# The first of two layers by a seven-product scheme, with its output kept in DRAM before the second layer

## The chip, the cores and the metric

The kernel runs on one core of one Trainium2 chip. The metric is the device time of one execution in microseconds. Five engines work side by side, each through its own list of instructions in order: TensorE (PE; PEld is its weight load), VectorE (DVE), ScalarE (ACT), GpSimd (POOL) and SyncE (SP, which here only issues DMAs). They wait for each other by semaphores.

## The reference

```
x: (8, 256, 1024) f32;  W0: (1024, 1024);  Wr: (8, 1024);  A: (8, 16, 1024);  B: (8, 1024, 16);  W1: (16, 1024, 1024)
logits = x @ Wr.T, plus 5 at expert lang_id[b];  gates = softmax of the two largest, 0 elsewhere
x1  = x  + x @ W0.T + 2 * sum over experts e of gates[e] * (x @ A[e].T) @ B[e].T
out = x1 + x1 @ W1[adapter[b]].T
```

Everything is f32. There are 2048 tokens of 1024 features. The two large products, x by W0 (the first layer) and x1 by the W1 that a row of 256 tokens picks (the second), have 2048 x 1024 x 1024 multiplications each.

## The kernel before

f32 operands are cut into a high part in fp32r and a low part (value minus high part), and a product is three matmuls: high by high, high by low, low by high. `load` (L244) brings a tile of 128 x 1024 numbers with four DMAs of 128 KB, each into 32 partitions (L255). GpSimd adds the identity to each weight tile (`add_ones`, L301, a 128x128 block), which gives the residual. VectorE transposes the tile (`turn`, L349), ScalarE copies out the high part (`high`, L487) and VectorE subtracts it from the tile (`low`, L356). A ring of four raw tiles and one of two turned tiles lie between them.

The work goes in four chunks of 512 tokens (two rows), by a loop of three turns and a last one written out. In each chunk TensorE makes `features` (x by A and Wr; L577 with 272 columns, L579 with 136), then eight `base_tile`s of 24 matmuls 128x512 each for W0 (L564 to L566) with `lora_tile`s of three, and then the second layer: eight output tiles of 24 matmuls, with x1 still in SBUF. From `features` VectorE works out the gates (`make_gates`, L398 to L436) and TensorE turns the gated features (L611). x1 leaves PSUM by `x1_high` (L507) and `x1_low` (L443). `put_out` (L517, L523) copies an output tile and stores it. W0 is loaded anew in each chunk, so the weights have 96 tiles in all (32 of W0, 64 of W1). The order of loads is a table (`FIRST`, `AFTER_GATES`, ..., `after_l1`).

Of the kernel before, what the change touches and what calls it, by code (L numbers as in the profile page):

```python
# [5 lines left out]
def cond_resid_kernel(nc, x, lang_ids, adapter_ids, w0, wr, a, b, w1, out):  # L25
    F32 = mybir.dt.float32
# [26 lines left out]

    WPC = M + BPC * M
    GROUPS = 3
    RING = GROUPS * KH
    RAW = 4
    BANKS = 7

    WARM = 37  # L60
    OUTS = 4
    L1_OUTS = NH * TT
    assert WPC % RING == 0 and ER == P and L1_OUTS % OUTS == 0 and M == 8 and L1_OUTS == 8

    AHEAD = 3
    FIRST = [("x", 0), ("a", 0)] + [("x", j) for j in range(1, XT)] + [("w", 0), ("w", 1), ("w", 2), ("b", 0)]
    AFTER_GATES = [("w", 3), ("w", 4)]
    AFTER_GATED = [("w", 5), ("w", 6), ("w", 7)]  # L70
    AFTER_L0 = [[], [], [("w", 8), ("w", 9)], [("w", 10), ("w", 11)], [("w", 12), ("w", 13)], [("w", 14), ("w", 15)],
                [("w", 16), ("w", 17)], []]

    def after_l1(j, last):
        own = [[18, 19], [20, 21], [22, 23], []][j]
        tokens = [[0, 1], [2, 3], [], []][j]
        following = [[], [], [0, 1], [2]][j]
        return [("w", n) for n in own] + ([] if last else [("x", t) for t in tokens] +
                                          [("w", WPC + n) for n in following])

    def body_order(last):
        return (AFTER_GATES + AFTER_GATED + [t for l in AFTER_L0 for t in l] +
                [t for j in range(NH) for t in after_l1(j, last)])
# [17 lines left out]
    with ctx:  # L101
# [564 lines left out]
```

## Time and profile before

| | us |
|---|---|
| median of 3 runs (lowest, highest) | 424.11 (423.76, 424.12) |
| the profiled execution, its span | 423.0 |
| PE busy / PEld busy | 414.4 / 349.1 |
| DVE busy | 314.1 |
| ACT busy | 163.1 |
| POOL busy | 59.5 |
| DMA | 68.52 MB, 162 GB/s over the span |

The profiled execution has only its span as a time of its own; it is 1.1 us shorter than the median of the runs. Busy time of PE counts overlapping matmuls, each of which is recorded at about 390 ns though the next starts earlier: the work of PE is read from the distance between starts.

### The profile page before, as it was taken

The numbers are of one execution on the slowest core, as the hardware profiler recorded it, in microseconds if no ns is written. First come the engines' busy times: TensorE is split into PE (matmuls) and PEld (weight loads), VectorE is DVE, ScalarE is ACT, GpSimd is POOL, SyncE is SP. The second block draws the span as 40 slices with busy tenths as digits, with TensorE's granted clock in tenths as the row PEclk, the third lists the DMA queues.
The fourth block names the chain that finished last, engine by engine and source line by source line (L and its number), as shares of the span: only waits on it lengthen the run. The fifth ranks groups of instructions, "written<-read, shape, count | busy, mean of one in ns | idle before, by whom it ended". The sixth has DMA issues, their size and how long they took to land.

```text
span 423.0 us, 6707 instructions
## 1 busy us (share of the span) xinstructions
PE 414.4 (98%) x1978; PEld 349.1 (83%) x1978; DVE 314.1 (74%) x378; ACT 163.1 (39%) x192; POOL 59.5 (14%) x104
## 2 busy tenths in 40 slices
PE   8898999999999999999999999999999999999996
PEld 8786888888898888888888888888889888888885
DVE  3999999999307999998615799999830799994410
ACT  3432544555212455454321445455421245533321
POOL 1021211201200121012110022111310012221000
PEclk9999999999999999999999999999999999999999
DMA  7994677797913666699650576679960356654111
GB/s 173 232 219 120 167 190 200 212 259 203 225 47 99 150 187 180 161 260 249 173 132 0 153 181 188 170 218 252 243 160 26 99 151 175 189 161 123 51 50 50
DMA packets 82542, 68.52 MB, mean 162 GB/s; under 512 B 7986, under 2 KB 82258, under 8 KB 82514
## 3 DMA queue, kind: packets, MB, share of 16 engines
q1 hardware_dynamic: 65618, 59.84, 55.3%
q10 hardware_dynamic: 16896, 8.39, 7.3%
q8 instruction: 8, 0.13, 0.1%
q14 instruction: 20, 0.16, 0.1%
HBM read 59.81 MB, written 8.39 MB: 161 GB/s over the span
## 4 chain that ended last, share of the span: by engine, by line
PE 89%; DVE 3%; DMA 2%; SPq 2%; issue 2%; ACT 0%; POOL 0%; DVEq 0%; ACTq 0%; POOLq 0%
PE banks L564 28%; PE banks L565 28%; PE banks L566 28%; PE banks L577 4%; SPq L255 2%; PE banks L579 1%; DMA raw<-in_L_cond_W_dram 1%; DMA raw<-in_x_dram 1%; DVE turned L349 1%; DVE turned L345 0%; DVE w_lo L356 0%; POOL raw L301 0%; PE gT_ps L611 0%; ACT w_hi L487 0%; DVE gT_lo L449 0%
## 5 line engine op out<-in xcount | busy, mean ns | idle before, releaser
L356 DVE TENSOR_TENSOR w_lo<-turned,w_hi 128x1024 fp32r<-128x1024 f32 x96 | 118.8, 1259 | 38.8 <-ACT w_hi L487 38.0
L487 ACT ACTIVATE w_hi<-turned 128x1024 fp32r<-128x1024 f32 x96 | 101.5, 1062 | 113.1 <-DVE turned L349 103.3
L349 DVE STREAM_TRANSPOSE turned<-raw 128x1024 f32<-128x1024 f32 x113 | 135.3, 1225 | 10.1 <-DMA raw<-in_x_dram 5.1
L301 POOL TENSOR_TENSOR raw<-raw,ident 128x128 f32<-128x128 f32 x96 | 58.4, 608 | 325.9 <-DMA raw<-in_L_cond_weight_dram 182.7
L564 PE MATMUL banks<-xT_hi,w_hi 128*128 128x512 f32 x256 | 100.2, 391 | 0.0
L565 PE MATMUL banks<-xT_lo,w_hi 128*128 128x512 f32 x256 | 99.7, 389 | 0.0
L566 PE MATMUL banks<-xT_hi,w_lo 128*128 128x512 f32 x256 | 99.6, 389 | 0.0
L564 PE MATMUL banks<-w_hi,x1T_hi 128*128 128x512 f32 x256 | 99.6, 389 | 0.0
L565 PE MATMUL banks<-w_lo,x1T_hi 128*128 128x512 f32 x256 | 99.6, 389 | 0.0
L566 PE MATMUL banks<-w_hi,x1T_lo 128*128 128x512 f32 x256 | 99.6, 389 | 0.0
L566 PEld LDWEIGHTS banks<-xT_hi,w_lo 128*128 128x128 f32 x256 | 48.1, 188 | 10.0
L564 PEld LDWEIGHTS banks<-w_hi,x1T_hi 128*128 128x128 f32 x256 | 48.1, 188 | 10.0
L565 PEld LDWEIGHTS banks<-w_lo,x1T_hi 128*128 128x128 f32 x256 | 48.1, 188 | 10.0
L566 PEld LDWEIGHTS banks<-w_hi,x1T_lo 128*128 128x128 f32 x256 | 48.1, 188 | 9.9
L565 PEld LDWEIGHTS banks<-xT_lo,w_hi 128*128 128x128 f32 x256 | 48.1, 188 | 9.7
L564 PEld LDWEIGHTS banks<-xT_hi,w_hi 128*128 128x128 f32 x256 | 48.1, 188 | 9.7
L517 ACT ACTIVATE out_stage<-banks 128x512 f32<-128x512 f32 x32 | 19.1, 597 | 71.3 <-PE banks L566 71.3
L577 PE MATMUL banks<-fac,xT_hi 128*128 128x272 f32 x128 | 30.7, 335 | 2.0 <-DVE fac L389 1.9
L579 PE MATMUL banks<-fac,xT_lo 128*128 128x136 f32 x128 | 29.0, 226 | 0.0
L577 PEld LDWEIGHTS banks<-fac,xT_hi 128*128 128x128 f32 x128 | 24.1, 188 | 2.5 <-DVE xT_lo L356 2.4
L443 DVE TENSOR_TENSOR x1T_lo<-banks,x1T_hi 128x512 fp32r<-128x512 f32 x32 | 21.2, 682 | 5.4 <-ACT x1T_hi L507 5.4
L398 DVE TENSOR_TENSOR h<-banks,h 128x544 f32<-128x544 f32 x4 | 2.9, 719 | 29.5 <-ACT h L499 29.5
(54 smaller groups left out, 197.8 us busy)
## 6 DMA issues: line engine op xcount, KB each, us to landing
raw<-in_L_cond_weight_dram SPq DMA_DIRECT2D x256, 128.0 KB, 2.7
raw<-in_L_cond_W_dram SPq DMA_DIRECT2D x128, 128.0 KB, 3.5
raw<-in_x_dram SPq DMA_DIRECT2D x64, 128.0 KB, 3.3
out_dram<-out_stage ACTq DMA_DIRECT2D x32, 256.0 KB, 3.1
raw<-in_L_cond_A_dram SPq DMA_DIRECT2D x4, 128.0 KB, 3.1
raw<-in_L_cond_B_dram SPq DMA_DIRECT2D x4, 128.0 KB, 4.5
gated<-in_L_cond_Wr_dram SPq DMA_DIRECT2D x4, 8.0 KB
lang_i<-in_itok_B_dram SPq DMA_DIRECT2D x1, 4.0 KB, 2.9
```

The lines of the kernel that those rows point to most:

```text
L255: sp.dma_start(raw[c * S:(c + 1) * S, s, :].rearrange("p (q j) -> p q j", q=Q), src[:, :, c * DQ:(c + 1) * DQ]).then_inc(raw_loaded[s], 16)
L301: nc.gpsimd.tensor_tensor(spot, spot, ident[:].rearrange("p (q j) -> p q j", q=Q), ALU.add)\
L349: nc.vector.transpose(turned[:, slot(item, ch, last, 2)].rearrange("p m (q s) -> p q m s", q=Q), raw[:, s, :].rearrange("p (q m j) -> p q ...
L356: nc.vector.tensor_tensor(dest(False, item), turned[:, slot(item, ch, last, 2)], dest(True, item).bitcast(F32), ALU.subtract)\
L443: nc.vector.tensor_tensor(x1T_lo[:, k, :], banks[:, l0_bank(k), :], x1T_hi[:, k, :].bitcast(F32), ALU.subtract).then_inc(x1_done, 1)
L487: nc.scalar.activation(dest(True, item), turned[:, slot(item, ch, last, 2)], ACT.Copy)\
L517: nc.scalar.activation(out_stage[:, s, :].rearrange("p (q k s) -> p q k s", q=Q, k=KH), banks[:, l1_bank(n), :].rearrange("p (k q s) -> p ...
L564: nc.tensor.matmul(ps, st_hi, mv_hi, start=start, stop=False)
L565: nc.tensor.matmul(ps, st_hi, mv_lo, start=False, stop=False)
L566: return nc.tensor.matmul(ps, st_lo, mv_hi, start=False, stop=stop)
L577: nc.tensor.matmul(banks[:, j, 0:2 * FC], xT_hi[:, m, t], fac[:, m, :, :].rearrange("p s f -> p (s f)"), start=m == 0, stop=False)
L579: mm = nc.tensor.matmul(banks[:, j, 0:FC], xT_lo[:, m, t], fac[:, m, 0, :], start=False, stop=m == M - 1)
```

## The change

The first layer is made once for the whole W0, in two spans of 1024 tokens. W0 (transposed, features by outputs) and the span's x are each cut into four quarters of 512 x 512. Four sums of W0's quarters (s1 to s4) and four of x's (t1 to t4) are formed, and seven products of quarters take the place of eight; `ORDER` gives their order. The products 1 and 2 use quarters without a sum; 6 is s2 by t2, 7 is s3 by t3, 5 is s1 by t1, 4 a quarter of W0 by t4, 3 is s4 by a quarter of x. With a for W0 and b for x the sums are s3 = a11 - a21, s2 = a22 - s3, s1 = a21 + a22, s4 = a12 - s2, t1 = b12 - b11, t2 = b22 - t1, t3 = b22 - b12, t4 = b21 - t2. All are made by GpSimd, with 128x512 instructions: 16 for W0, 16 for the x of each span. The four quarters of x1 come out of PSUM by further copies and additions (`copy_p1`, `copy_u2`, `copy_u3`, `add_p1`, `add_up`), are cut into high and low part in a stage of two places, and are written to a DRAM tensor `x1_kept` (`keep`). The second layer follows after both spans, row by row: `load_x1` reads a row's high and low parts back with two DMAs of 1 MB, issued by ScalarE; W1's tiles come through five raw places and three groups of four tiles. `features` is now one f32 matmul of 136 columns per block in place of the two fp32r ones. The loops are written out.

```diff
+    ORDER = (1, 2, 6, 7, 5, 4, 3)
...
+    LOADS = ([("a",)] + [x_item(0, 0, t) for t in range(XT)] + [("w", m) for m in range(HM)] +
+             [x_item(0, 1, t) for t in range(XT)] + [("w", m) for m in range(HM, M)] + [("b",)] +
+             [x_item(1, h, t) for h in range(2) for t in range(XT)])
...
+    x1_kept = nc.dram_tensor("x1_kept", [M, P, 2, NB * T], F32, kind="Internal").ap()
...
+            def keep(s, quarter, r):
+                e = quarter_at(s, quarter, r)
+                m = r + (HM if quarter[0] == "2" else 0)
+                t0 = s * 2 * HALF + (HALF if quarter[1] == "2" else 0)
+                sp.wait_ge(x1_lo_done, e + 1)
+                sp.dma_start(x1_kept[m, :, :, t0:t0 + HALF], stage[:, e % 2].rearrange("p (h f) -> p h f", h=2))\
+                    .then_inc(kept[e % 2], 16)
...
+            def make_t1(s, t):
+                pool.wait_ge(transposed, TURN_AT[x_item(s, 1, t)] + 1)
+                pool.wait_ge(featured, featured_at(s, 0, t) + 1)
+                pool.wait_ge(lo_done, PIECE_AT[("x", 1, 1, HM - 1) if s else ("xt", t)] + 1)
+                nc.gpsimd.tensor_tensor(half_x(0, t, 0), half_x(1, t, 0), half_x(0, t, 0), ALU.subtract)\
+                    .then_inc(t1_done, 1)
...
+            def make_s3(r):
+                pool.wait_ge(transposed, TURN_AT["w", HM + r] + 1)
+                pool.wait_ge(lo_done, PIECE_AT["wt", r] + 1)
+                a11, a21 = quarter_w(7, r), quarter_w(5, r)
+                nc.gpsimd.tensor_tensor(a11, a11, a21, ALU.subtract).then_inc(s3_done, 1)
+            def make_s2(r):
+                pool.wait_ge(s3_done, r + 1)
+                nc.gpsimd.tensor_tensor(s2_sum(r), quarter_w(4, r), quarter_w(7, r), ALU.subtract).then_inc(s2_done, 1)
+            def make_s1(r):
+                a21, a22 = quarter_w(5, r), quarter_w(4, r)
+                nc.gpsimd.tensor_tensor(a21, a21, a22, ALU.add).then_inc(s1_done, 1)
+            def make_t2(s, k):
+                if s == 0:
+                    pool.wait_ge(t1_done, k + 1)
+                    dst, b22, t1 = t2_by_tile(k, 1, ring_f), half_x(1, k, 1), half_x(0, k, 0)
+                    b22, t1 = (v.rearrange("p (m f) -> p m f", m=HM) for v in (b22, t1))
+                else:
+                    pool.wait_ge(t1_done, 2 * XT)
+                    pool.wait_ge(steps, k_end(*UNITS[UNIT_AT[1, 6, k, 1] - RING][0:3]))
+                    dst, b22, t1 = unit(1, 6, k, 1, ring_f), quarter_x(1, HM + k), quarter_x(0, k)
+                nc.gpsimd.tensor_tensor(dst, b22, t1, ALU.subtract).then_inc(t2_done, 1)
+            def make_t4(s, k):
+                pool.wait_ge(t2_done, s * HM + k + 1)
+                if s == 0:
+                    t2, b21 = t2_by_tile(k, 1, ring_f), half_x(0, k, 1).rearrange("p (m f) -> p m f", m=HM)
+                else:
+                    t2, b21 = unit(1, 6, k, 1, ring_f), quarter_x(0, HM + k)
+                nc.gpsimd.tensor_tensor(b21, b21, t2, ALU.subtract).then_inc(t4_done, 1)
+            def make_s4(r):
+                pool.wait_ge(s2_done, r + 1)
+                a12 = quarter_w(3, r)
+                nc.gpsimd.tensor_tensor(a12, a12, s2_sum(r), ALU.subtract).then_inc(s4_done, 1)
+            for m in range(HM):
+                add_ones(("w", m))
+            for t in range(XT):
+                make_t1(0, t)
+                make_t2(0, t)
+                make_t4(0, t)
+            for r in range(HM):
+                add_ones(("w", HM + r))
+                make_s3(r)
+                make_s2(r)
+                make_s4(r)
+            for t in range(XT):
+                make_t3(0, t)
+            for r in range(HM):
+                make_s1(r)
+            for t in range(XT):
+                make_t1(1, t)
+            for t in range(XT):
+                make_t3(1, t)
+            for k in range(HM):
+                make_t2(1, k)
+                make_t4(1, k)
+            for n in range(NW1):
+                add_ones(("w1", n))
...
+            def load_x1(row):
+                if row == 0:
+                    act.wait_ge(steps, product_end(1, 4))
+                elif row == 1:
+                    act.wait_ge(steps, product_end(1, 3))
+                else:
+                    act.wait_ge(l1_ready, (row - 1) * 2 * TT)
+                for slot in range(2):
+                    act.wait_ge(kept[slot], (8 if row < NB // 2 else 16) * 16)
+                for low in range(2):
+                    act.dma_start(x1_part(row, low).bitcast(F32),
+                                  x1_kept[:, :, low, row * T:(row + 1) * T].rearrange("m p t -> p m t"))\
+                        .then_inc(x1_loaded[row % 2], 16)
...
+            def step(s, i, k, r, bank, first):
+                ps = bank.rearrange("p (t f) -> p t f", t=XT)
+                u_hi, u_lo = (u_part(i, r, low)[:, k * P:(k + 1) * P] for low in range(2))
+                x_hi, x_lo = x_part(s, i, k, 0), x_part(s, i, k, 1)
+                nc.tensor.matmul(ps, u_hi, x_hi, start=first and k == 0, stop=False, skip_group_check=True)
+                nc.tensor.matmul(ps, u_hi, x_lo, start=False, stop=False, skip_group_check=True)
+                nc.tensor.matmul(ps, u_lo, x_hi, start=False, stop=k == HM - 1, skip_group_check=True)\
+                    .then_inc(steps, 1)
...
+            def span(s):
+                product(s, 6, lambda r: pe.wait_ge(p1_copied, HM * s + r + 1), False, main_bank)
+                turn_gated(s)
+                product(s, 7, lambda r: pe.wait_ge(u2_copied, HM * s + r + 1), False, main_bank, range(HM - 1))
+                pe.wait_ge(gT_done, s + 1)
+                pe.wait_ge(lo_done, PIECE_AT["b",] + 1)
+                for r in range(HM):
+                    pe.wait_ge(p1_added, HM * s + r + 1)
+                    lora(s, "11", r)
+                product(s, 7, None, False, main_bank, range(HM - 1, HM))
+                product(s, 5, lambda r: pe.wait_ge(summed_up, added_at(s, "11", r) + 1), True, side_bank)
+                for r in range(HM):
+                    lora(s, "22", r)
+                product(s, 4, lambda r: pe.wait_ge(u3_copied, HM * s + r + 1), False, main_bank)
+                for r in range(HM):
+                    lora(s, "21", r)
+                product(s, 3, lambda r: pe.wait_ge(summed_up, added_at(s, "22", r) + 1), False, side_bank)
+                pe.wait_ge(lo_done, PIECE_AT["bd",] + 1)
+                for r in range(HM):
+                    lora(s, "12", r)
...
+            features(0, 0)
+            for _ in range(FILL):
+                nc.tensor.matmul(banks[:, 0, 0:P], ident[:], ident[:], start=True, stop=True)
+            first_products()
+            span(0)
+            features(1, 0)
+            features(1, 1)
+            product(1, 1, lambda r: pe.wait_ge(summed_up, added_at(0, "12", r) + 1), True, main_bank)
+            product(1, 2, lambda r: pe.wait_ge(h_copied, 3 + r // 2), True, side_bank)
+            span(1)
```

GpSimd, at the start. Before, it only adds the identity to weight tiles (`raw`), three of them ahead of the loop:

```order
L285 IOTA iota_i 128x8
L287 AFFINE_SELECT ident<-ident 128x128
L301 TENSOR_TENSOR raw<-raw,ident 128x4x32 x3
L311 UNCONDITIONAL_BRANCH
L311 ISA
L301 TENSOR_TENSOR raw<-raw,ident 128x4x32 x3
```

After; `tokens_f` is x transposed, `ring_f` holds t2, `turned_w_f` W0 transposed, `weights_f` s2 (the rows begin with the first four weight tiles and end within the second one of the other four):

```order
L490 TENSOR_TENSOR tokens_f<-tokens_f,ring_f 128x512
L451 TENSOR_TENSOR tokens_f<-tokens_f 128x512
L482 TENSOR_TENSOR ring_f<-tokens_f 128x4x128
L490 TENSOR_TENSOR tokens_f<-tokens_f,ring_f 128x512
L444 TENSOR_TENSOR raw<-raw,ident 128x4x32
L463 TENSOR_TENSOR turned_w_f<-turned_w_f 128x512
L467 TENSOR_TENSOR weights_f<-turned_w_f 128x512
L495 TENSOR_TENSOR turned_w_f<-turned_w_f,weights_f 128x512
L444 TENSOR_TENSOR raw<-raw,ident 128x4x32
L463 TENSOR_TENSOR turned_w_f<-turned_w_f 128x512
```

Between the identity of W0's fourth tile and that of the fifth there are now twelve sums of x, and between the fifth and the sixth three sums of W0.

ScalarE, in the second layer. Before, between two output tiles (`out_stage` to DRAM) it makes high parts for W and x:

```order
L517 ACTIVATE out_stage<-banks 128x512
L523 ISA
L523 DMA out_dram<-out_stage 512x1x128
L476 REGISTER_ALU
L487 ACTIVATE xT_hi<-turned 128x8x128
L476 REGISTER_ALU
L487 ACTIVATE xT_hi<-turned 128x8x128
L515 REGISTER_ALU
L517 ACTIVATE out_stage<-banks 128x512
L523 ISA
L523 DMA out_dram<-out_stage 512x1x128
```

After; `tokens<-x_kept` are the two DMAs that read a row of x1 back:

```order
L948 ACTIVATE turned_w<-weights_f 128x8x128 x2
L959 ACTIVATE sums<-banks 128x512
L965 DMA out_dram<-sums 512x1x128
L937 DMA tokens<-x_kept 128x8x256 x2
L948 ACTIVATE weights<-weights_f 128x8x128 x2
L959 ACTIVATE sums<-banks 128x512
L965 DMA out_dram<-sums 512x1x128
L948 ACTIVATE weights<-weights_f 128x8x128 x2
```

A row's x1 is now asked for on ScalarE's queue behind the last output tile of the row two before it.

## Rows read from the trace of the kernel before

**Rows 1.** The page, part 1 (engine, busy us, share), and the PEclk row

```profile
PE 414.4 (98%) x1978; PEld 349.1 (83%) x1978; DVE 314.1 (74%) x378; ACT 163.1 (39%) x192; POOL 59.5 (14%) x104
PEclk9999999999999999999999999999999999999999
```

**Rows 2.** The page, part 4: the chain that ended last, shares by engine

```profile
PE 89%; DVE 3%; DMA 2%; SPq 2%; issue 2%; ACT 0%; POOL 0%; DVEq 0%; ACTq 0%; POOLq 0%
```

**Rows 3.** Timeline of PE, second layer: start, length (us), what; 44 matmuls between

```profile
104.56 0.39 PE L564 MATMUL banks<-w_hi,x1T_hi 128*128 128x512 f32 x1
...
114.76 0.39 PE L564 MATMUL banks<-w_hi,x1T_hi 128*128 128x512 f32 x1
```

**Rows 4.** Timeline of PE, features: first pair, and the one seven pairs later

```profile
14.82 0.39 PE L577 MATMUL banks<-fac,xT_hi 128*128 128x272 f32 x1 [1.89 <-DVE fac L389]
15.10 0.34 PE L577 MATMUL banks<-fac,xT_hi 128*128 128x272 f32 x1
...
16.76 0.33 PE L577 MATMUL banks<-fac,xT_hi 128*128 128x272 f32 x1
```

**Rows 5.** Windows of L561: stretch, length, PE busy (records), PEld, PEclk, DMA, GB/s

```profile
3.00:5.00 2.00, 2.00 (x11) 2.00 (x11) 1.00 0.79 188
9.00:11.00 2.00, 2.00 (x21) 2.00 (x20) 1.00 0.93 188
```

**Rows 6.** The chain of waits in order of time, its end: start, length, what

```profile
419.05 0.24 PE banks L566
419.31 0.60 ACT out_stage L517
```

**Rows 7.** The chain of waits, the turning of the gated features

```profile
136.12 0.44 PE gT_ps L611 x4
```

**Rows 8.** Groups of instructions by form: count | busy us, mean ns | idle before

```profile
L349 DVE STREAM_TRANSPOSE turned<-raw 128x1024 f32<-128x1024 f32 x113 | 135.3, 1225 | 10.1 <-DMA raw<-in_x_dram 5.1 <-DMA raw<-in_L_cond_A_dram 1.4 <-POOL raw L301 1.2
L356 DVE TENSOR_TENSOR w_lo<-turned,w_hi 128x1024 fp32r<-128x1024 f32 x96 | 118.8, 1259 | 38.8 <-ACT w_hi L487 38.0
L301 POOL TENSOR_TENSOR raw<-raw,ident 128x128 f32<-128x128 f32 x96 | 58.4, 608 | 325.9 <-DMA raw<-in_L_cond_weight_dram 182.7 <-DMA raw<-in_L_cond_W_dram 143.3
L443 DVE TENSOR_TENSOR x1T_lo<-banks,x1T_hi 128x512 fp32r<-128x512 f32 x32 | 21.2, 682 | 5.4 <-ACT x1T_hi L507 5.4
L507 ACT ACTIVATE x1T_hi<-banks 128x512 fp32r<-128x512 f32 x32 | 18.0, 591 | 13.9 <-PE banks L566 13.9
L283 POOL MEMSET gated<- 128x256 f32 x1 | 0.3, 312 | 0.3 <-POOLq L653 0.3
L284 POOL MEMSET ident<- 128x128 f32 x1 | 0.2, 206 | 0.0
```

**Rows 9.** GpSimd line L301: duration ns min/median/max

```profile
L301 POOL TENSOR_TENSOR raw<-raw,ident x96: 454/464/1471, 17.8 to 385.5; 128x128 f32<-128x128 f32 x96
```

**Rows 10.** Timeline of all engines, start

```profile
1.68 11.25 PE L561 MATMUL gT_ps<-ident 128*128 128x128 f32 x74 [1.68 <-POOL ident L287]
5.10 1.25 DVE L349 STREAM_TRANSPOSE turned<-raw 128x1024 f32<-128x1024 f32 x1 [5.10 <-DMA raw<-in_x_dram]
11.93 1.85 SPq L255 DMA_DIRECT2D raw<-in_L_cond_W_dram  x4
17.82 0.58 POOL L301 TENSOR_TENSOR raw<-raw,ident 128x128 f32<-128x128 f32 x1 [16.19 <-DMA raw<-in_L_cond_W_dram]
```

**Rows 11.** Timeline of DVE, gates of the third chunk

```profile
227.28 0.19 DVE L400 TENSOR_TENSOR logits<-h,bias 128x32 f32<-128x32 f32 x1 [0.16 <-DVE h L398]
227.62 0.36 DVE L408 MAX8 top<-logits 128x8 f32<-128x8 f32 x4
230.29 0.69 DVE L436 TENSOR_TENSOR gated<-h,gates 128x512 f32<-128x512 f32 x1
```

**Rows 12.** Windows of all engines; DMA share and GB/s stand last

```profile
13.00:22.00 9.00, 7.05 (x57) 6.90 (x58) 8.63 (x9) 3.44 (x4) 1.37 (x2) 1.00 1.12 232
88.00:94.00 6.00, 6.00 (x28) 4.97 (x27) 5.79 (x6) 3.67 (x4) 0.00 (x0) 1.00 1.07 256
108.00:111.00 3.00, 3.00 (x15) 2.49 (x14) 0.26 (x1) 0.00 (x0) 0.46 (x1) 1.00 0.97 289
```

More of the change, by code:

```diff
@@ L55, in cond_resid_kernel, with x_item @@
+    def x_item(s, h, t):
+        return ("x", s, h, t)
     GROUPS = 3
[L56 to L60, printed above, removed]
+    NW1 = NB * M
+    L1_OUTS = NB * 2 * TT
     OUTS = 4
[L62 to L70, printed above, removed]
@@ L281, in _ @@
+            load_w1(10)
+            keep(1, "12", 2)
+            load_w1(11)
+            keep(1, "12", 3)
+            for n in range(12, NW1):
+                load_w1(n)
         @block.gpsimd
@@ L372, in _ @@
+            turn(x_item(0, 0, 1))
+            low(("xt", 0))
             dve.wait_ge(consts, 3)
@@ L459, in _ @@
[L459 to L465 removed]
+            turn(x_item(0, 0, 3))
+            low(("xt", 2))
+            turn(("w", 0))
+            low(("xt", 3))
+            turn(("w", 1))
+            low(("wt", 0))
+            turn(("w", 2))
+            low(("wt", 1))
+            turn(("w", 3))
+            low(("wt", 2))
@@ new lines, in _ @@
+            span(0)
+            low(("x", 1, 1, 0))
+            low(("x", 1, 1, 1))
+            turn(x_item(1, 1, 0))
+            for r in range(HM):
+                add_up(0, "12", r)
+            turn(x_item(1, 1, 1))
+            x1_low(0, "12", 0)
+            x1_low(0, "12", 1)
+            turn(x_item(1, 1, 2))
+            low(("x", 1, 1, 2))
+            low(("x", 1, 1, 3))
+            turn(x_item(1, 1, 3))
+            x1_low(0, "12", 2)
+            x1_low(0, "12", 3)
+            make_gates(1)
@@ new lines, in highs, with copy_h @@
+            def highs(kind, *which):
+                for r in range(HM):
+                    high((kind, *which, r))
+            def copy_h(s, h):
+                act.wait_ge(featured, featured_at(s, h, XT - 1) + 1)
+                if s:
+                    for slot in range(2):
+                        act.wait_ge(kept[slot], 8 * 16)
+                nc.scalar.activation(h_all[:, h * XT:(h + 1) * XT, :].rearrange("p (k i) f -> p k (i f)", i=2),
+                                     features_of(s, h), ACT.Copy).then_inc(h_copied, 1)
@@ new lines, in _ @@
+            span(0)
+            high(("x", 1, 1, 0))
+            high(("x", 1, 1, 1))
+            x1_high(0, "12", 0)
+            x1_high(0, "12", 1)
+            high(("x", 1, 1, 2))
+            high(("x", 1, 1, 3))
+            x1_high(0, "12", 2)
+            x1_high(0, "12", 3)
+            copy_h(1, 0)
+            copy_h(1, 1)
+            exponentials(1)
+            highs("x", 1, 2)
+            for r in range(HM):
+                copy_p1(1, r)
+            high(("x", 1, 6, 0))
+            high(("x", 1, 6, 1))
@@ new lines, in _ @@
+            high(("x", 1, 6, 2))
+            high(("x", 1, 6, 3))
+            high(("x", 1, 7, 0))
+            high(("x", 1, 7, 1))
+            for r in range(HM):
+                copy_u2(1, r)
+            gT_high(1)
+            high(("x", 1, 7, 2))
+            high(("x", 1, 7, 3))
+            span(1)
+            high_w1(5)
+            load_x1(1)
+            x1_high(1, "12", 0)
+            x1_high(1, "12", 1)
+            high_w1(6)
+            high_w1(7)
+            x1_high(1, "12", 2)
```

1174 lines of the change are left out of this document (763 added, 411 removed).

## The prediction

> **What bounds the kernel now.** I read the page first. TensorE is busy 98% of the span and VectorE 74% [rows 1]; the chain that ended last runs through PE for 89% [rows 2]. So nearly each microsecond is TensorE's work, and what TensorE does not have to do comes off the time, as long as it is fed. Two matmuls overlap in the records, so the price of one is the distance between starts: 45 steps from 104.56 to 114.76 us, 0.2267 us for 512 columns [rows 3]. A pair of the features' matmuls takes (16.76 - 15.10) / 7 = 0.237 us [rows 4]. TensorE begins its features at 14.82 us [rows 4] and ends at 419.3 [rows 6]; 3.7 us of store follow to 423.0. Its work sums to 1632 x 0.2267 = 370.0, 128 x 0.237 = 30.3 and 16 turns at 0.11 = 1.8 [rows 7], 402.1 us in all, so in those 404.5 us it stood still only 2.4. The start, 14.8 us, and that are all that a better feed could win.
>
> **TensorE's work after.** Seven products in two spans are 7 x 2 x 4 x 4 x 3 = 672 matmuls of 512 columns where 768 were: 672 x 0.2267 = 152.3 us. The LoRA keeps its 96 (21.8), the second layer its 768 (174.1), the turns 1.8. The features become 128 f32 matmuls of 136 columns. An f32 matmul leaves two records, and 21 of 128 columns start in 2.00 us [rows 5]: 0.095 per record, 0.19 to 0.20 per matmul, 0.21 for 136 columns, 27.2 us in all. The sum is 377.2 us, 24.9 less. That is the whole gain.
>
> **The start: GpSimd's sums.** Product 6 cannot start before s2 of all four row blocks, and nothing is queued on TensorE that could go ahead of it. What lies before it on TensorE is features (6.8), product 1 (10.9), features (6.8), product 2 (10.9): 35.4 us.
>
> Loads. The first tile is turned from 5.10 to 6.35 us [rows 10]. With three raw slots a slot is used again after 1.85 us of issue, the landing (issued by 13.78, seen by GpSimd at 17.82: 4.04) [rows 10] and a turn of 1.25: about 7.3 us for three tiles, 2.45 each. x's fifth tile is the tenth loaded: 6.35 + 9 x 2.45 = 28.4 us. The last x tile follows at about 36, so product 1 ends near 32 and product 2 near 49.
>
> The price of a sum of 512 columns on GpSimd is in no row. The nearest is L301, 128 columns, 454 ns at least and 608 on average [rows 8, 9]. From below: two memsets of 256 and 128 columns take 312 and 206 ns [rows 8], 100 ns of which is fixed; if 200 were fixed here, 512 columns would cost 0.20 + 4 x 0.254 = 1.22 us. From above: 4 x 0.454 = 1.82, or 4 x 0.608 = 2.4 when VectorE gets in the way (a record of 1471 ns shows that it can) [rows 9]. With 100 ns fixed it is 0.10 + 4 x 0.354 = 1.52, and I take 1.5, the overhead nearest to a row.
>
> The Trainium skill (GPSIMD Engine Reference, Elementwise: side-by-side cycle accounting) states about 2.6 cycles an element at 1.2 GHz for two inputs. By it this sum would cost an estimated 1.1 us plus dispatch, and the chain below would be about 7 us shorter; L301's 454 ns for 128 columns, with the same rate, leaves 0.18 us for dispatch, so the row doesn't contradict it.
>
> GpSimd's queue, in order, from 28.4 us: 12 sums of x; then for each of W0's last four row blocks the identity (0.46), the turn on VectorE that waits for it (1.25, with 0.2 of signals), and s3, s2, s4, which wait for that turn; the next identity is queued behind s4. Up to the last s2 that is 12 + 3 x 3 + 2 = 23 sums, 34.5 us, four times 1.91 = 7.6, and 23 signals of about 0.05: 43.3. s2 is ready at 71.7; ScalarE's high part (0.59) and VectorE's low part (0.68) [rows 8] with signals bring 73.3 us. TensorE has been idle since 49, for 24 us.
>
> After such a rest the clock. After the rest ahead of the program only 11 records of L561 start in 2 us where later 21 do [rows 5], though the profile gives a granted clock of 1.00, its 2.4 GHz level, in both. All 74 take 11.25 us [rows 10], and would take 74 x 0.095 = 7.0 at the later pace: a restart costs at most 4.2 us, at least nothing if the clock holds. I charge 3.0. Product 6 ends at 73.3 + 10.9 + 3.0 = 87.2. The gates of 1024 tokens wait for product 7's first pieces, which wait for t3, behind the last s4: 71.7 + 5 x 1.5, 79.5, and 2 us of cutting. The chunk's gates take 3.7 us [rows 11], with twice as many maxima and indices about 5.2: done at 86.9, just covered by product 6.
>
> **The rest of the first layer.** In span 0 VectorE has per product about four sums from PSUM, four low parts of x1, four of W0 and four of x: 16 x 0.68 = 10.9 us against 13.6 of TensorE (a product with its LoRA), so it keeps up with little to spare; without W0's parts in span 1, more. Stage and `kept` waits add a few microseconds where VectorE and ScalarE are in order behind a store, and the second gates have 10.9 us of product 1 to hide in and need 10 to 12. I charge 3.0 us for all of that. The copies on ScalarE (12 per span at 0.59) and the second half of GpSimd's sums lie beside products. W0 being loaded once (24 tiles less for VectorE, 60 us) is worth nothing, as VectorE was not the bound.
>
> **The second layer: DMA.** It now has no first layer between to fetch in. A row has 96 matmuls, 21.8 us, for which come 4.19 MB of W1, 2.10 of x1 and 1.05 of output: 7.34 MB, 337 GB/s. When it starts nine W1 tiles have been brought; up to its last group it still needs 55 tiles (28.8 MB), seven rows of x1 (14.7), the last four `keep`s (2.1) and 28 outputs (7.3), 52.9 MB. Of its 174.1 us, 159 are left for that when the last group (10.9) and some 4 us of landing, turning and cutting are taken off: 333 GB/s to be hidden. The rows show: loads alone 232 GB/s with the DMA engines full (share 1.12), loads with stores 256 at a share of 1.07, and 289 at 0.97 for 3 us [rows 12]. From below 256 gives 52.9 / 0.256 + 15 = 222 us, 48 more than TensorE's. From above 289 x 1.12 / 0.97 = 334 hides it all. I take 289 / 0.97 = 298, the mixed stretch that is nearest to this traffic, taken to a full engine: 177.5 + 15 = 192.5 us, 18.4 more. VectorE needs 2 x 1.24 us per tile, 8 tiles in 19.9 us of a row's 21.8, and is not the bound.
>
> The Trainium skill (DMA: Bandwidth & Descriptors, Measured) gives 341 GB/s for a transfer of 1 MB, the size of `load_x1`'s. By it x1's 14.7 MB would take an estimated 43 us in place of 49 and the layer 6 us less; no row here shows so large a transfer.
>
> **The sum.** 73.3 + (377.2 - 35.4 = 341.8) + 3.0 + 3.0 + 18.4 + 3.7 = 443.2 us against the execution's own 423.0; the runs' median lies 1.1 above it: **444 us**.
>
> **Rivals.**
> (a) The sums as above, but the second layer keeps TensorE's pace. For it: the loads' 232 GB/s go into 32 partitions at a time, and x1 comes over all 128; a stretch with stores was already at 289. Against it: 333 was held nowhere. 444 - 18.4 = 425.6 us, within 5 of it.
> (b) Faster: the 24.9 us of matmuls saved outweigh the late start. It is one mechanism, a sum at its lower price on GpSimd, and it counts only where (a) holds too: with 1.22 us the chain is 23 x 0.28 = 6.4 us shorter, 419.2 us. It decides below 1.43 us a sum (425.6 - 424.1 = 1.5 us, over 23). For it speaks the L301 median of 464 ns, hardly above its minimum; against it that VectorE is denser at the start than elsewhere.
> (c) Both go badly: GpSimd and VectorE shut each other out (L301 at 608 on average, 1.3 times its median, which makes a sum 1.95 us and the chain 10 us longer), or DMA stays at 256 GB/s (30 more): 454 to 480 us, 465 as its middle.
>
> **Chances.** Forecast 0.50; (a) 0.22; (b) 0.12; (c) 0.16. A change under 0.2%, 0.85 us, can't be told from none: of (a), 0.06 falls on the faster side and 0.04 within. Faster 0.18, within 0.04, slower 0.78. The likeliest case's own range is 434 to 453. The range runs from 416, under (b), to 467 in (c); outside lie the outer half of (c) and the very good starts.
>
> **What would show it.** Right: product 6's first matmul at 66 to 79 us behind an idle stretch of 15 to 28 us that ends with GpSimd's s2; 512-column sums at 1.4 to 1.7 us; 672 matmuls less idle than 25 us saved; in the second layer DMA share above 0.95 and PE waiting for `x1_kept` or W1 tiles, with the layer 185 to 200 us long. Wrong: product 6 within 5 us of product 2's end, or a second layer of 174 to 178 us; then the time is at or under 424. If the first-layer products have gaps of over 10 us beside the one ahead of product 6, my 3.0 for the rest was the step that failed.

## The result, and the profile after

The changed kernel takes **465.16 us** (median of 4 runs, 464.17 to 467.46) against 424.12 for the kernel before in the same comparison: a ratio of 1.097, 95% interval 1.094 to 1.100. It is slower by 41 us; the forecast was 444, slower by 20. The profiled execution spans 462.6 us where the sum said 443.2.

The page of the changed kernel: part 1, and the granted clock, DMA share and GB/s in 40 slices of 11.6 us. They answer to [rows 1].

```profile
PE 405.7 (88%) x1920; PEld 339.0 (73%) x1920; DVE 301.5 (65%) x380; ACT 167.1 (36%) x239; POOL 112.9 (24%) x128
PEclk9999956999999999999999959997999999999999
DMA  8974220014247680005578989999999999999921
GB/s 193 218 206 115 87 74 23 0 46 183 91 142 222 230 222 6 0 1 201 164 247 249 301 248 280 261 295 310 281 319 304 321 301 308 308 306 316 253 69 45
```

TensorE fell from 98% to 88% of a longer span. The DMA row swings between 0 and 9 in the first layer and stands at 8 or 9 from the 22nd slice to the 38th: the second layer. The chain that ended last, by engine, to be set against [rows 2]: TensorE's 89% has become 26%, and DMA leads.

```profile
DMA 29%; PE 26%; DVE 17%; POOL 9%; SPq 9%; issue 6%; ACT 2%; ACTq 2%; DVEq 0%; POOLq 0%
```

What TensorE's lines waited for in the changed kernel (total us, times, longest):

```profile
PE banks L1106 <- DVE weights L562: 20.7, 2, 20.3
PE banks L1203 <- DMA tokens<-x_kept: 12.4, 5, 5.4
PE banks L1203 <- DVE weights L657: 11.1, 1, 11.1
PE banks L1126 <- DVE stage L613: 4.0, 1, 4.0
PE banks L1203 <- issue: 2.3, 1, 2.3
```

L1106 waits ahead of product 6 and L1126 for the gates, both at the start. L1203 is the second layer: 11.1 us for tiles of W1, 12.4 us in five waits for x1 and 2.3 us that the profile puts down to nothing. These seven waits are 25.8 us. Here are the matmuls behind the longest three, from the timeline of PE (start, length, what, idle before):

```profile
73.67 0.77 PE L1106 MATMUL banks<-ring,weights 128*128 128x512 f32 x1 [20.26 <-DVE weights L562]
...
90.25 1.89 PE L1126 MATMUL banks<-ident,stage 128*128 128x128 f32 x8 [3.99 <-DVE stage L613]
...
274.20 0.80 PE L1203 MATMUL banks<-weights,tokens 128*128 128x512 f32 x1 [11.06 <-DVE weights L657]
```

Set against the forecast's own steps, in the profiled execution:

| step | forecast, us | measured, us |
|---|---|---|
| product 6 begins | 73.3 | 73.67 |
| product 6, with the clock's restart | 13.9 | 12.6 |
| wait for the gates | 0 | 4.0 |
| from there to the second layer | 159.8 | 162.0 |
| second layer (252.2 to 458.9) | 192.5 | 206.7 |
| tail | 3.7 | 3.7 |
| sum | 443.2 | 462.6 |

Of the 19.4 us, 14.2 are the second layer's. Its 206.7 us are 32.6 more than its matmuls need (174.1): 25.8 are the waits, and the 6.8 that are left go by subtraction to the slower matmuls behind them.

### The profile page after: what moved, and what is told of

Same layout as the page of the kernel before. It is cut to its first block, busy times and chain, and to the rows that moved or that the text cites. A ratio compares the mean times of both kernels' runs of the same rounds, so it can differ in the third digit from the quotient of the medians.

```text
span 462.6 us, 6010 instructions
## 1 busy us (share of the span) xinstructions
PE 405.7 (88%) x1920; PEld 339.0 (73%) x1920; DVE 301.5 (65%) x380; ACT 167.1 (36%) x239; POOL 112.9 (24%) x128
## 4 chain that ended last, share of the span: by engine, by line
DMA 29%; PE 26%; DVE 17%; POOL 9%; SPq 9%; issue 6%; ACT 2%; ACTq 2%; DVEq 0%; POOLq 0%
DMA raw<-in_L_cond_weight_dram 13%; SPq L359 8%; DMA x_kept<-stage 6%; PE banks L1106 5%; PE banks L1108 5%; PE banks L1107 5%; DMA tokens<-x_kept 4%; PE banks L1203 3%; PE banks L1205 3%; PE banks L1204 3%; DVE weights_f L651 3%; DMA ring_f<-in_L_cond_weight_dram 2%; DVE stage L641 2%; DVE turned_w_f L544 2%; DMA raw<-in_x_dram 2%
## 5 line engine op out<-in xcount | busy, mean ns | idle before, releaser
L1106 PE MATMUL banks<-ring,weights 128*128 128x512 f32 x192 | 76.5, 399 | 20.6 <-DVE weights L562 20.3
L1203 PE MATMUL banks<-weights,tokens 128*128 128x512 f32 x176 | 71.0, 404 | 21.9 <-DVE weights L657 11.1
L651 DVE STREAM_TRANSPOSE weights_f<-raw 128x1024 f32<-128x1024 f32 x42 | 52.0, 1240 | 34.9 <-POOL raw L444 34.7
L1204 PE MATMUL banks<-weights,tokens 128*128 128x512 f32 x176 | 70.3, 399 | 0.0
L1205 PE MATMUL banks<-weights,tokens 128*128 128x512 f32 x176 | 70.2, 399 | 0.0
L948 ACT ACTIVATE weights<-weights_f 128x1024 fp32r<-128x1024 f32 x44 | 46.0, 1058 | 60.4 <-DVE weights_f L651 43.3
L657 DVE TENSOR_TENSOR weights<-weights_f,weights 128x1024 fp32r<-128x1024 f32 x44 | 52.6, 1195 | 10.7 <-ACT weights L948 10.6
L1106 PEld LDWEIGHTS banks<-ring,weights 128*128 128x128 f32 x192 | 36.8, 191 | 28.8 <-DVE weights L562 20.7
L1203 PEld LDWEIGHTS banks<-weights,tokens 128*128 128x128 f32 x176 | 34.3, 195 | 31.1 <-DMA tokens<-x_kept 12.6
L1107 PE MATMUL banks<-tokens,weights 128*128 128x512 f32 x128 | 50.2, 392 | 0.0
L1108 PE MATMUL banks<-ring,turned_w 128*128 128x512 f32 x128 | 50.1, 392 | 0.0
L1205 PEld LDWEIGHTS banks<-weights,tokens 128*128 128x128 f32 x176 | 34.1, 194 | 7.3
L1204 PEld LDWEIGHTS banks<-weights,tokens 128*128 128x128 f32 x176 | 34.2, 194 | 7.0
L1203 PE MATMUL banks<-turned_w,tokens 128*128 128x512 f32 x80 | 31.5, 394 | 3.9 <-issue 2.3
L651 DVE STREAM_TRANSPOSE weights_f<-ring_f 128x1024 f32<-128x1024 f32 x22 | 27.3, 1239 | 7.2 <-POOL ring_f L444 7.2
L451 POOL TENSOR_TENSOR tokens_f<-tokens_f 128x512 f32<-128x512 f32 x8 | 11.9, 1507 | 80.9 <-DVE ring L562 76.0
L1204 PE MATMUL banks<-turned_w,tokens 128*128 128x512 f32 x80 | 31.2, 390 | 0.0
```

What stands on the lines that cost most here:

```text
L651: nc.vector.transpose(w1_turn(n).rearrange("p (m q s) -> p q m s", m=M, q=Q), raw_tile(SLOT[item]).rearrange("p (q m j) -> p q m j", q=Q, ...
L657: nc.vector.tensor_tensor(w1_dest(n, 1), w1_turn(n).rearrange("p (m f) -> p m f", m=M), w1_dest(n, 0).bitcast(F32), ALU.subtract).then_inc ...
L948: nc.scalar.activation(w1_dest(n, 0), w1_turn(n).rearrange("p (m f) -> p m f", m=M), ACT.Copy)\
L1106: nc.tensor.matmul(ps, u_hi, x_hi, start=first and k == 0, stop=False, skip_group_check=True)
L1107: nc.tensor.matmul(ps, u_hi, x_lo, start=False, stop=False, skip_group_check=True)
L1108: nc.tensor.matmul(ps, u_lo, x_hi, start=False, stop=k == HM - 1, skip_group_check=True)\
```

## Experiments

Spans below are of profiled executions; the changed kernel's is 462.6. Its four executions spanned 462.4, 462.6, 464.2 and 465.6 us, and each run below but the last was executed once, so a change of the total under some 3 us can't be told from chance; single waits inside a profile say more. The kernel before took 424.2 to 425.9 us beside these runs.

### Where the start's 20 us come from

**Run 1: W0's sums s3, s2, s4 on VectorE**

```diff
                 add_ones(("w", HM + r))
-                make_s3(r)
-                make_s2(r)
-                make_s4(r)
...
             turn(("w", 4))
+            sums_w(0)
```

`sums_w(r)` makes the same three subtractions of a block on VectorE; one such call stands behind the turn of each of the tiles 4 to 7.

> The changed kernel, with W0's sums s3, s2 and s4 (12 of the 48) made by VectorE right behind the turn of their tile; GpSimd keeps all of x's and s1. Theory (product 6 waits for GpSimd's queue, and each sum in it counts at about 1.36 us): of GpSimd's chain behind 47.0 us only four identities, four turns and VectorE's sums at about 0.7 us remain, 4 x (0.46 + 1.4 + 2.1) less the last s4, so s2 is ready at about 62 and product 6 starts at 63 to 65 in place of 73.7: 8 to 11 us off the time, 452 to 455. Rival (VectorE, or the loads, would hold it anyway): product 6 stays within 3 us of 73.7.

457.8 us, span 456.0. Product 6 began at 72.99, hardly earlier: the theory's 63 to 65 failed. Timeline of VectorE in run 1, its sums for one block of W0 and the next (L647, L649, L651):

```profile
52.81 0.69 DVE L647 TENSOR_TENSOR turned_w_f<-turned_w_f 128x512 f32<-128x512 f32 x1
...
57.63 1.23 DVE L527 STREAM_TRANSPOSE turned_w_f<-raw 128x1024 f32<-128x1024 f32 x1
58.89 1.70 DVE L647 TENSOR_TENSOR turned_w_f<-turned_w_f 128x512 f32<-128x512 f32 x1
60.63 1.63 DVE L649 TENSOR_TENSOR weights_f<-turned_w_f 128x512 f32<-128x512 f32 x1
62.30 1.64 DVE L651 TENSOR_TENSOR turned_w_f<-turned_w_f,weights_f 128x512 f32<-128x512 f32 x1
```

The same instruction takes 0.69 us at 52.81 and 1.70 at 58.89. In between, at 53.77, GpSimd began its sums t3 and s1. So my price held only while GpSimd stood still. Nearly all of the 6.6 us came from elsewhere: product 6 gave 0.7, the wait for the gates, which was gone, 4.0, and the slow matmuls behind that wait 1.7 (from the turning of the gated features to the LoRA 9.0 us where the changed kernel took 10.7).

**Run 5: run 1, with GpSimd's t3 and s1 behind VectorE's last s4**

```diff
+            pool.wait_ge(s4_done, HM)
             for t in range(XT):
                 make_t3(0, t)
```

> As the run with W0's sums on VectorE, but GpSimd's t3 and s1 of the first span wait until VectorE has made the last s4. There VectorE's 512-column sums took 0.69 us while GpSimd stood still and 1.6 to 1.75 while it worked. Theory (two instructions that read two SBUF operands don't run at once on the two engines, each waits for the other's to end): with GpSimd still, all of VectorE's take 0.7, and product 6 starts at 63 to 66 in place of 73.0; t3 comes later, so the gates' gap returns (3 to 5 us) and the time falls by 3 to 7, to about 449 to 453. Rival (the longer instructions come from a semaphore wait counted in, or from the operands' place): they stay at 1.6 and product 6 at 73.

457.41 us, span 455.6. The timeline of VectorE in run 5, the same three sums, with GpSimd idle:

```profile
56.94 0.69 DVE L648 TENSOR_TENSOR turned_w_f<-turned_w_f 128x512 f32<-128x512 f32 x1
57.66 0.69 DVE L650 TENSOR_TENSOR weights_f<-turned_w_f 128x512 f32<-128x512 f32 x1
58.39 0.69 DVE L652 TENSOR_TENSOR turned_w_f<-turned_w_f,weights_f 128x512 f32<-128x512 f32 x1
...
64.73 2.83 DVE L546 TENSOR_TENSOR weights<-weights_f,weights 128x512 fp32r<-128x512 f32 x2
```

That GpSimd's sums are what makes VectorE's long is thereby shown, and the rival is out. Product 6 began at 67.67, a little later than expected: the last two low parts (2.83 us) fell beside the GpSimd that had been let go. The total missed the 449 to 453: it gained only 0.4 us on run 1, for the wait for the gates was back with 2.65 us, and the second layer, which began 2.9 us earlier, lasted 2.5 longer.

**Run 2: W0's identities added before its sums**

```diff
+            for m in (4, 5, 6):
+                add_ones(("w", m))
             for r in range(HM):
-                add_ones(("w", HM + r))
                 make_s3(r)
                 make_s2(r)
                 make_s4(r)
+                if r == 1:
+                    add_ones(("w", 7))
```

> The changed kernel with all sums on GpSimd; only its order is another: the identities of W0's fifth, sixth and seventh tiles stand ahead of the first s3, that of the eighth behind the second tile's sums. Theory (in the chain of 24 us for W0, GpSimd stands idle 1.36 us four times for the turn of the tile whose identity it has just added): three of the four waits go, and product 6 starts at 68 to 70 in place of 73.7, the time is 4 to 6 us less, 457 to 459. Rival (the sums' own time is all that counts): under 2 us.

458.59 us, span 456.8. Product 6 at 68.69, 5.0 us earlier, and the time both as expected. In the changed kernel GpSimd had stood 1.36 us before each of four s3, waiting for a turn that it had itself just released.

**Run 6: run 5, with those identities between x's sums**

```diff
                 make_t4(0, t)
+                if t:
+                    add_ones(("w", HM + t - 1))
+            add_ones(("w", 7))
```

> As the run before it, with the identities of W0's last four tiles put between GpSimd's sums of x, so that VectorE turns and sums W0's tiles while GpSimd still sums x. Theory: the two engines together have from 29.6 us 12 sums of 1.3, 12 of 0.7, four cuts and ten turns, of which only the turns overlap: product 6 at 58 to 63, the stall under 10 us, time 443 to 448. Rival (nothing overlaps any more once GpSimd and VectorE alternate): product 6 not before 64, no gain over the run before it.

453.49 us, span 451.7. Product 6 at 63.54, 10.1 us earlier than in the changed kernel, though each engine's sums took 1.6 to 1.8 us while both worked. Sharing the sums gained 3.9 us on run 5, against the rival, but the time is over the theory's 443 to 448: product 6 came just behind the 58 to 63, the wait for the gates stayed at 3.0, and the second layer took its 207 us.

### Where the second layer's 14 us come from

**Run 4: rows 3 to 8 of x1 read back to one eighth.** The rest of these rows is missing from the result.

```diff
+                n = 1 if row >= 2 else M
-                    act.dma_start(x1_part(row, low).bitcast(F32),
+                    act.dma_start(x1_part(row, low)[:, 0:n].bitcast(F32),
```

> The changed kernel, which for rows 3 to 8 reads back only one of eight feature blocks of x1 (128 KB in place of 1 MB per DMA), so 11 of the layer's 53 MB are left out. Theory (rows wait 1.5 to 5.4 us each for x1 to come back, because it is asked for when its place is free and then takes 15 to 20 us beside W1's tiles): the waits ahead of the later rows go and each row takes 21.9 us, while the 11 us gap stays: 449 to 452. Rival (W1's loads alone are too slow): rows wait for W1 tiles instead and less than 5 us go.

448.77 us, span 447.0: 15.6 less, as the theory said. Windows of run 4 (length; PE, PEld, DVE, ACT, POOL busy; clock, DMA share, GB/s):

```profile
252.00:291.00 39.00, 24.63 (x102) 19.65 (x101) 21.27 (x23) 10.88 (x14) 4.29 (x8) 0.87 0.99 270
291.00:443.00 152.00, 152.00 (x672) 125.69 (x670) 120.33 (x103) 69.01 (x80) 34.74 (x50) 1.00 0.94 230
```

From 291 on TensorE is busy without a break: 672 matmuls in 152 us, the 0.227 of [rows 3]. The first 39 us, with 24.6 busy, are nearly as in the changed kernel (25.6); the gap there is still 12.21 us.

**Run 3: W1's tiles 6 to 8 issued ahead of x1's stores**

```diff
-            keep_all(1, "21")
             for n in range(EARLY, EARLY + RAW):
                 load_w1(n)
+            keep_all(1, "21")
```

> The changed kernel with the loads of W1's tiles 7 to 9 issued ahead of the last span's four keeps of the lower left quarter instead of behind them. Theory (the 11.1 us in which TensorE stood still 11 us into the second layer came from SP's order, its loads being queued behind keeps that wait for x1's low parts, and not from DMA's rate): the gap falls under 3 us and the second layer, 206.7 us long, becomes 194 to 198: 452 to 455. Rival (DMA's rate of about 305 GB/s sets the layer's length whatever the order): the gap's time comes back as longer waits for x1 or W1 in the rows behind, and the layer stays over 203 us.

(Tiles are counted from 0 here; the expectation counts them from 1.) 463.79 us, span 462.0. The rival was right: the layer took 205.7 us. In run 3's timeline ScalarE, which must issue row 2's reload, waits for the stores that are now later:

```profile
255.39 0.60 ACT L925 ACTIVATE stage<-banks 128x512 fp32r<-128x512 f32 x1 [16.21 <-DMA x_kept<-stage]
```

It had waited 9.17 us. The gap shrank from 11.06 to 7.53 and another of 1.06 opened; the total moved by 0.6, which is nothing.

**Run 7: the second span keeps 64 of 512 tokens, and rows 5 to 8 read the places of rows 1 to 4.** Those rows come out otherwise than in the reference.

```diff
+                n = 64 if s else HALF
-                sp.dma_start(x1_kept[m, :, :, t0:t0 + HALF], ...
+                sp.dma_start(x1_kept[m, :, :, t0:t0 + n], ...
```

> The changed kernel with the second span's 16 keeps writing 64 of 512 tokens each (64 KB in place of 512), and rows 5 to 8 reading back the places of rows 1 to 4: 7.3 MB less to write, of which most just ahead of the second layer. Theory (x1's low parts wait for the two-place stage, the stage for keeps on a full DMA, and SP's W1 loads for them in turn; this loop makes the 11 us gap): ScalarE's waits of 9 us for x_kept go, W1's tiles 7 and 8 are issued 8 to 10 us earlier and the gap falls under 4 us: 448 to 453. Rival (the tiles are late because 4 MB of x1's first rows and W1 share the DMA at its rate): over 7 us of gap stay.

460.12 us, span 458.3: the gap fell to 6.20 and the span by 4.3. The gap lies between the theory's 4 and the rival's 7, and the time far over the theory's 448 to 453. Tiles 6 to 8 were issued at 247.4 in place of 251.3, so the stores are some half of the gap.

**Run 9: row 2's reload behind W1's tile 6**

```diff
             high_w1(5)
-            load_x1(1)
...
             high_w1(6)
+            load_x1(1)
             high_w1(7)
```

> Row 1's reload of x1 (2.1 MB) is issued behind the high part of W1's tile 6 instead of 1.5 us ahead of tiles 6 to 8. Theory (those 2.1 MB are what delays tile 6, and the layer as a whole is bound by its bytes): the gap of 11.06 us shrinks to 4 to 6 us, but most of that comes back in the later waits for x1, and the span falls by less than 2 us (460.6 to 462.6). Rival (the early gap is a fault of order alone): the gap shrinks as much, the later gaps stay as they are, and the span falls by 5 us or more, to 457.6 or under.

463.79 us, span 462.0. ("Row 1" there is `load_x1(1)`, the second row.) Timeline of PE in run 9, its first three gaps of the layer:

```profile
266.67 0.80 PE L1203 MATMUL banks<-weights,tokens 128*128 128x512 f32 x1 [4.44 <-DVE weights L657]
...
284.96 0.77 PE L1203 MATMUL banks<-turned_w,tokens 128*128 128x512 f32 x1 [5.56 <-issue]
...
315.75 0.80 PE L1203 MATMUL banks<-weights,tokens 128*128 128x512 f32 x1 [6.18 <-DMA tokens<-x_kept]
```

11.06 became 4.44, 2.33 became 5.56, 5.43 became 6.18, and the later waits grew by another 0.9: most was given back, as expected of a stretch that its bytes bound. The same shows over all runs: from the first layer's end to its own, the second layer took 206.8 us in the changed kernel and 205.7 to 210.0 in each of the eight runs that leave nothing out, whatever their order and start.

**Run 8: the reload of row r + 2 issued ahead of row r's last output**

```diff
-                put_out(o)
                 if o % (2 * TT) == 2 * TT - 1 and o // (2 * TT) + 2 < NB:
                     load_x1(o // (2 * TT) + 2)
+                put_out(o)
```

> The changed kernel with the reload of a row's x1 issued ahead of the copy and store of the output tile that ends the row, not behind them, about 1.7 us earlier. Theory (rows wait for x1 because it is asked for late and then takes its time): the waits of 1.5 us ahead of rows 5 to 7 go, five to seven us in all: 456 to 458. Rival (DMA is full at 306 GB/s, so an earlier issue only moves the wait to W1's tiles): the time falls by less than 2 us.

468.19 us, span 466.4: 3.8 more, and my theory was wrong; the rival's "by less than 2 us" holds, as nothing was gained. x1's reloads landed in 13.1 us where they had taken 15.0, and outputs in 10.7 where they had taken 8.8. Whether the order cost anything is open: the changed kernel itself spanned up to 465.6.

### Together

**Run 10: run 6 with the cuts of runs 4 and 7** (the parts of x1 that those leave out are missing)

> The shared start (W0's sums on VectorE, GpSimd held, identities between x's sums) together with an eighth of the reload for rows 3 to 8, and span 2 keeping 64 of 512 tokens, with rows 5 to 8 reading the places of rows 1 to 4; the output is not the reference's. Theory (the losses of the start and of the second layer are independent, and the rest is TensorE's work): the savings add up, layer 2 starts at about 241 us, lasts 183 to 188 us, and the span is 428 to 432 us, still 5 to 9 above the execution before. Rival (they hide each other): span 437 us or more.

428.9 us, span 427.1. Windows of run 10, from the 274th us on:

```profile
274.00:423.00 149.00, 149.00 (x659) 123.38 (x658) 116.21 (x101) 67.74 (x78) 33.16 (x49) 1.00 0.92 228
```

The single savings sum to 10.9 + 15.6 + 4.3 = 30.8 us, the run saved 35.5: the losses do not hide each other, and the rival's 437 is out. The 4.7 us between the sums show no more than that, since each saving is counted from 462.6; counted from 465, which the changed kernel reached too, they agree. And the run is still 4.1 us over the 423.0 of the execution before, with most of x1's traffic left out. Product 6 begins at 63.8, 13.6 later than 14.8 us of start and 35.4 of work would allow, and the second layer takes 184.0 us for 174.1 of matmuls; with the wait for the gates (2.8) that alone eats the matmuls saved.

**Run 11: runs 6 and 9 together, nothing left out**

> The shared start and row 1's reload behind tile 6, nothing left out: the best complete version by the runs so far. Theory (layer 2 is bound by its bytes): 0 to 2 us under the shared start's span of 451.7, a median near 452 us, 6 to 7% slower than the kernel before. Rival (order alone): 447 us or less.

453.95 us (453.12 to 455.05, four executions), ratio 1.070, interval 1.068 to 1.073: 7% slower than the kernel before. Its span of 452.2 is 0.5 above run 6's where the theory said 0 to 2 below, so moving the reload gained nothing here; the rival's 447 is excluded. Runs 6 and 11 are the best complete versions found, and can't be told apart.

## Why the prediction was right in kind and short by half

The direction and the two places were right: a start that waits for GpSimd, and a second layer bound by its bytes. The size was not: 41 us where 20 were forecast, and 465 lies outside the 434 to 453 of the likeliest case. It is the middle of rival (c), but by luck: neither of (c)'s conditions held, since GpSimd's chain was shorter than worked out and DMA held 297 GB/s and not 256. Three terms of the sum failed: the bytes left when the second layer starts, its tail, and the gates "just covered by product 6".

**The start was right in its number, by errors that cancel.** The timeline of POOL in the changed kernel, the first sums and one s3:

```profile
29.63 2.18 POOL L451 TENSOR_TENSOR tokens_f<-tokens_f 128x512 f32<-128x512 f32 x1 [4.83 <-DVE tokens_f L544]
31.89 1.30 POOL L482 TENSOR_TENSOR ring_f<-tokens_f 128x512 f32<-128x512 f32 x1
33.27 1.29 POOL L490 TENSOR_TENSOR tokens_f<-tokens_f,ring_f 128x512 f32<-128x512 f32 x1
...
48.86 1.65 POOL L463 TENSOR_TENSOR turned_w_f<-turned_w_f 128x512 f32<-128x512 f32 x1 [1.36 <-DVE turned_w_f L544]
...
68.86 1.59 POOL L467 TENSOR_TENSOR weights_f<-turned_w_f 128x512 f32<-128x512 f32 x1
```

A sum undisturbed takes 1.27 to 1.30 us, 1.6 when VectorE is in the way. From 29.63 to the last s2's end at 70.45 are 40.8 us, 2.5 under the 43.3 worked out. It began 1.2 us later than said, and from there to product 6 it took 3.2 us where 1.6 were charged. "Product 6 cannot start before s2" named one sum too few. The low part of s2 is written over s2, which s4 still reads, so VectorE waits for the last s4 as well (L552, `dve.wait_ge(s4_done, ...)`), and s4 ran from 70.53 to 71.80. The timeline of VectorE:

```profile
71.91 1.67 DVE L562 TENSOR_TENSOR weights<-weights_f,weights 128x512 fp32r<-128x512 f32 x1 [2.57 <-POOL turned_w_f L495]
```

This low part, beside GpSimd's t3, took 1.67 us where the one at 67.01 had taken 0.65. The Trainium skill (GPSIMD Engine Reference, Elementwise: side-by-side cycle accounting) with its 2.6 cycles an element made an estimated 1.1 us plus dispatch: the trace agrees, with 1.27. (With the 0.18 us for dispatch that the prediction itself works out, the chain would be 5 us shorter by that figure, not 7.) Rival (b)'s lower price was thus real, and decided nothing, as the second layer did not keep TensorE's pace.

**The clock was nearly right.** 3.0 us were charged, 1.7 came (12.6 for product 6 less 10.9). Windows of the changed kernel around product 6, and behind the 5.4 us gap in the second layer (clock third from the end):

```profile
55.00:73.00 18.00, 0.00 (x0) 0.00 (x0) 7.53 (x9) 3.77 (x7) 14.79 (x13) 0.53 0.29 88
73.70:79.70 6.00, 6.00 (x20) 4.88 (x21) 6.00 (x5) 1.15 (x2) 6.00 (x5) 0.75 0.01 4
79.70:85.80 6.10, 6.10 (x28) 5.05 (x28) 6.07 (x14) 0.00 (x0) 4.73 (x3) 1.00 0.00 0
...
317.00:323.00 6.00, 6.00 (x15) 4.76 (x16) 4.37 (x5) 1.55 (x2) 2.20 (x3) 0.54 1.13 322
323.00:341.00 18.00, 18.00 (x81) 14.89 (x81) 14.14 (x13) 8.71 (x10) 4.62 (x7) 1.00 1.12 280
```

The rest leaves the clock near its 1.2 GHz level; 20 matmuls start in the first 6 us, 28 in the next. What I did not charge is that the waits of the second layer pay this too: the row behind the 5.4 us gap took 24.6 us where others took 22.0.

**"Done at 86.9, just covered by product 6" failed: 4.0 us.** (Its own terms, 71.7 + 5 x 1.5 + 2 + 5.2, make 86.4.) The gates' 5.2 us were right (84.90 to 90.19), and t3 was done at 77.6, before the 79.5 worked out. VectorE reached the gates late: the low parts of product 7's operands, queued ahead, ran beside GpSimd's t3 and s1. The same four instructions in the timeline of VectorE, in the changed kernel, and ahead of them an addition that reads PSUM:

```profile
67.58 0.68 DVE L623 TENSOR_TENSOR sums<-banks,sums 128x512 f32<-128x512 f32 x1
...
74.70 6.89 DVE L562 TENSOR_TENSOR turned_w<-turned_w_f,weights 128x512 fp32r<-128x512 f32 x4
```

and in run 1, where GpSimd had finished:

```profile
74.01 2.48 DVE L545 TENSOR_TENSOR turned_w<-turned_w_f,weights 128x512 fp32r<-128x512 f32 x4
```

I had the mutual exclusion in rival (c), as a price on GpSimd's sums; its larger price fell on VectorE's instructions, 1.72 us for 0.62. The Trainium skill (SBUF — State Buffer, SBUF: two separate sides) calls the shared pair of ports an exclusive lock and "not a bandwidth split", taken by VectorE's instructions with two inputs in SBUF when GpSimd reads SBUF. The trace agrees that two inputs in SBUF are what matters: in run 1 the transposition at 57.63, with one input, keeps its 1.23 us beside GpSimd's sums, and L623, with one operand from PSUM, takes its usual 0.68 beside the s3 that GpSimd ran from 67.16 to 68.78. That one engine waits out the whole of the other's instruction is not shown as such: side by side, a pair of them takes 1.72 us, a little less than 0.62 + 1.27 one after the other.

**The rest of the first layer** was 2.2 us longer than said. The features' matmul took (20.63 - 13.21) / 32 = 0.232 us where 0.21 were forecast, which is 1.4 of it on the 64 that lie behind product 6; 0.8 is what is left, 3.8 for the 3.0 charged. Of these 3.8, 1.7 are the slow matmuls behind the wait for the gates, which the comparison with run 1 showed: a second restart of the clock that the sum had no term for.

```profile
13.21 7.58 PE L1099 MATMUL banks<-fac,tokens_f 128*128 128x136 f32 x64
...
20.63 2.84 PE L1177 MATMUL banks<-ident 128*128 128x128 f32 x24
```

**The second layer failed in its bytes and its tail, not in its rate.** Windows of the changed kernel, to be read against [rows 12]:

```profile
252.20:437.00 184.80, 158.99 (x674) 128.85 (x673) 138.39 (x123) 74.75 (x88) 36.18 (x58) 0.95 1.09 297
...
344.00:367.50 23.50, 22.00 (x97) 17.90 (x97) 18.08 (x16) 9.30 (x12) 3.87 (x8) 1.00 1.12 313
...
437.00:459.00 22.00, 21.86 (x96) 17.75 (x95) 3.14 (x3) 3.44 (x6) 0.00 (x0) 1.00 0.20 58
```

297 GB/s over the stretch was the 298 taken. That they agree is in part luck: 298 was worked out for a share of 1.00, the measured share is 1.09, and rows of the layer at 1.11 to 1.12 lie anywhere from 278 to 313 GB/s. But 184.8 us at 297 are 54.9 MB, where I had 52.9. The sentence that failed is "When it starts nine W1 tiles have been brought": six had been. Tiles 6 to 8 (1.6 MB) stand on SP's queue behind four stores of x1, and I had followed the raw slots, not the queue:

```profile
242.25 8.90 SPq L390 DMA_DIRECT2D x_kept<-stage  x4
251.34 7.20 SPq L359 DMA_DIRECT2D raw<-in_L_cond_weight_dram  x12
```

With them the 52.9 MB become 54.5, and the stretch took 184.8 us where 177.5 were charged, 7.3 more. The other 7 are the tail: I took off the last group and its landing, 15 us, but DMA is low from 437 on, and behind that stands the last row's 21.9 us whole, since a row starts only when its x1 is there. Inside the layer the same missing tiles make the 11.06 us gap. In the timelines of POOL and ACT:

```profile
263.19 0.45 POOL L444 TENSOR_TENSOR raw<-raw,ident 128x128 f32<-128x128 f32 x1 [22.82 <-DMA raw<-in_L_cond_weight_dram]
```

```profile
248.06 0.60 ACT L925 ACTIVATE stage<-banks 128x512 fp32r<-128x512 f32 x1 [9.17 <-DMA x_kept<-stage]
...
249.58 0.42 ACTq L937 DMA_DIRECT2D tokens<-x_kept  x1
```

ScalarE waited for a store to free the stage and then put row 2's reload, 2.1 MB, just ahead of tile 6, which GpSimd saw only 11.9 us after its issue. Runs 3, 7 and 9 each moved one of these three parties, and the full engines moved the wait to another. Run 4 shows the size of the whole: with rows 3 to 8 cut, the layer runs at TensorE's pace from 291 on. Of the signs named ahead, the DMA share above 0.95 and product 6 at 66 to 79 us came; the layer's 206.7 us is outside the 185 to 200, and the wait for product 6 ended with s4, not s2.

Three things stay open: how the 11 us divide between stores and reload beyond run 7's half; whether the reload's form (pieces of 256 tokens, 1 KB each, x1 being stored feature by feature) limits its rate, since run 4 took bytes and pieces away together; and what a complete version would take that keeps x1 as one f32 in place of two parts, with half the traffic. The last two were not tried.

## What to carry to other kernels

Work saved on the bounding engine is worth its time only if its feed is ready: here 25 us of matmuls were bought with 20 us of standing still ahead of product 6, 4 ahead of the gates and 33 us in the second layer. When an operand is written over the place of another, every reader of the old one is on the path too: here s4. When intermediates go through DRAM, sum the bytes per stage, count from what each queue has really issued when the stage starts, and add the last unit of work whole behind the last landing. When GpSimd gets long two-input work, price VectorE's two-input instructions beside it at two to three times their own time, and look first at what waits for them.

## What the runs showed of the hardware that was not expected

- A VectorE subtraction of 512 columns with both inputs in SBUF takes 0.69 us with GpSimd idle and 1.63 to 1.75 with GpSimd adding; GpSimd's sum goes from 1.27 to 1.6 or 1.8.
- Loads of 1 MB, tile loads and stores together moved 306 to 313 GB/s from 344 us on at a DMA share of 1.12 (278 and 295 in two earlier rows of x1 at the same share or 0.01 less), where loads of tiles alone had 232 [rows 12]. One megabyte landed 15.0 us after its issue (median).
- A rest of TensorE of 5.4 us was enough for a clock of 0.54 in the next 6 us, and cost 2.6 us.
